# Seven block products in place of eight for the second layer of the last 32 steps instead of the last 24

## The reference

```
xW = einsum('ntd,dg->ntg', x, Wx) + b                 # 256 -> 1024
a = xw_t + prev_h @ Wh                                # per step, 256 -> 1024
next_c = sigmoid(f) * prev_c + sigmoid(i) * tanh(g)
next_h = sigmoid(o) * tanh(next_c)

h = concatenate([h, -h], axis=-1)
h = s0 * (h @ sign(k0)); h = relu(h) * 2              # 512 -> 1024
h = s1 * (h @ sign(k1)); h = relu(h) * 2              # 1024 -> 1024
h = s2 * (h @ sign(k2))                               # 1024 -> 256
y = x + h
```

## Time and profile before

| | |
|---|---|
| median of 3 runs | 272.96 us (272.89 to 273.32) |
| the profiled execution | 273.06 us, of it 271.2 us from the first to the last instruction |
| TensorE busy | 267.2 us of the 271.2 (99%), 3568 matmuls |
| VectorE, ScalarE, GpSimd busy | 215.4 us, 174.6 us, 48.1 us |
| the first step of the recurrence begins | 19.09 us |
| the last piece of fill ends, the part behind the loop begins | 223.02 us |
| granted TensorE clock | 1.00 |

### The profile page before, as it was taken

How to read it: one execution, slowest core, us unless ns; L and a number is a source line. 1 busy time by engine, 2 the same in 40 slices (tenths; PEclk the granted TensorE clock), 3 DMA queues, 4 the chain that set the end, 5 groups by cost and what they waited for, 6 DMA issues and landing times.

```text
span 271.2 us, 8903 instructions
## 1 busy us (share of the span) xinstructions
PE 267.2 (99%) x3568; PEld 219.9 (81%) x3568; DVE 215.4 (79%) x769; ACT 174.6 (64%) x522; POOL 48.1 (18%) x70
## 2 busy tenths in 40 slices
PE   8999999999999999999999999999999999999995
PEld 6888888878999999999998899998887676666563
DVE  3878888888888888888888888887777777997355
ACT  4789786878566667655765576556777867733320
POOL 0010000012211112331222102000222225603030
PEclk9999999999999999999999999999999999999999
DMA  7980000000000000000010001000000010100003
GB/s 210 346 342 1 4 2 0 2 4 2 2 0 4 4 2 22 22 2 5 2 42 0 2 4 41 2 2 4 4 0 2 2 42 0 41 0 0 2 0 116
DMA packets 5432, 8.72 MB, mean 32 GB/s; under 512 B 656, under 2 KB 3472, under 8 KB 5264
## 3 DMA queue, kind: packets, MB, share of 16 engines
q1 hardware_dynamic: 5104, 7.64, 8.1%
q10 hardware_dynamic: 288, 0.52, 0.5%
HBM read 6.07 MB, written 2.10 MB: 30 GB/s over the span
## 4 chain that ended last, share of the span: by engine, by line
PE 98%; DVE 1%; POOL 0%; issue 0%; POOLq 0%
PE WK L555 36%; PE WK L538 14%; PE G L517 11%; PE WK L573 10%; PE G L508 10%; PE ACC L587 6%; PE G L573 4%; PE WK L604 2%; PE ACC L604 1%; PE G L649 1%; PE G L538 1%; PE ACC L538 1%; DVE x L886 1%; PE G L555 0%; POOL zero L1094 0%
## 5 line engine op out<-in xcount | busy, mean ns | idle before, releaser
L555 PE MATMUL WK<-h,k 128*128 128x256 f16 (+1 forms) x856 | 107.7, 276 | 0.0
L555 PEld LDWEIGHTS WK<-h,k 128*128 128x128 fp8e5 x856 | 80.8, 98 | 11.3 <-issue 0.2
L814 ACT ACTIVATE tT<-aT 128x128 f32<-128x128 f32 x126 | 39.0, 310 | 44.6 <-DVE aT L1033 43.4
L1033 DVE TENSOR_REDUCE aT<-G 128x128 f32<-128x256 f32 x128 | 48.2, 418 | 7.7 <-PE G L517 6.3
L701 ACT ACTIVATE G<-xw 128x256 f32<-128x256 f32 x126 | 46.6, 370 | 0.0
L538 PE MATMUL WK<-xs,wxs 128*128 128x512 f32 x168 | 42.5, 400 | 0.0
L517 PE MATMUL G<-h,w 128*128 128x64 f16 x1008 | 39.5, 192 | 0.0
L508 PEld LDWEIGHTS G<-h,w 128*128 128x128 f16 x1008 | 32.9, 96 | 6.7 <-DVE h L1050 5.1
L538 PEld LDWEIGHTS WK<-xs,wxs 128*128 128x128 f32 x168 | 30.4, 188 | 5.9
L508 PE MATMUL G<-h,w 128*128 128x32 f16 x1008 | 35.2, 177 | 0.0
L517 PEld LDWEIGHTS G<-h,w 128*128 128x128 f16 x1008 | 33.2, 97 | 0.0
(11 more groups left out here) (116 smaller groups left out, 283.9 us busy)
## 6 DMA issues: line engine op xcount, KB each, us to landing
x<-in_x SPq DMA_DIRECT2D x3, 512.0 KB, 8.4
out_y<-x SPq DMA_DIRECT2D x10, 128.0 KB, 1.8
xw<-in_wh SPq DMA_DIRECT2D x4, 256.0 KB, 5.0
k<-in_k SPq DMA_DIRECT2D x1, 1024.0 KB, 10.2
out_y<-x SPq DMA_DIRECT2D x4, 192.0 KB, 1.9
x<-in_x ACTq DMA_DIRECT2D x2, 256.0 KB, 3.6
xw<-in_wx SPq DMA_DIRECT2D x4, 128.0 KB, 4.0
xw<-in_wx SPq DMA_DIRECT2D x2, 256.0 KB, 5.2
```

Of the source, the lines that this page charges most:

```text
L555: ins = eng.matmul(layer_src(tile), w, rhs, start=a == 0, stop=last)
L814: eng.activation(tT[:, B * j0:B * j1], aT[:, j0:j1].rearrange("p j b -> p (j b)"), ACT.Tanh, scale=half_gain0 if t == 0 else half_gain).th ...
L1033: eng.tensor_reduce(aT[:, j0:j1], G[g][:, 0:256].rearrange("p (j h b) -> p j b h", h=2, b=B), op=ALU.add, axis=AX.X).then_inc(added[g])
```

## The change

The portions become four of 8 steps and two of 16 steps, so that the seven products cover the last 32 steps. A wide portion has 512 columns, a whole PSUM bank. With this:

- `N1`, `N2` are 4 and 5, `NW` is 512; the second layer of steps 32 to 39, which was a portion of its own with 128 matmuls of 256 columns, is now part of the seven products;
- `fill(t)` is 2.03 for every step from 1 on, where it was 2.2 to 2.3;
- the first layer of portion `N1` is spread over other steps, and p1 and p2 change places with its last tiles; one matmul of p2 moves behind the loop;
- the terms tq of products 5 and 6, and t23, move from xw and h1 to memory that xs and wxs leave free, and those of product 4 into b1; ScalarE waits for the last x product or for p2 before it writes them;
- h1 keeps a size of its own, and the copies of p1 wait for the seed of step 39 instead of step 31.

```
-CHUNKS = ((0, 8), (8, 8), (16, 8), (24, 8), (32, 8), (40, 12), (52, 12))
-N1, N2 = 5, 6
+CHUNKS = ((0, 8), (8, 8), (16, 8), (24, 8), (32, 16), (48, 16))
+N1, N2 = 4, 5
...
 def fill(t):
-    return 3.4 if t < 0 else 1.8 if t < 1 else 2.3 if t < 9 else 2.2 if t < 16 else 2.3
+    return 3.4 if t < 0 else 1.8 if t < 1 else 2.03
...
 def act_cost(tile):
-    return 0.48 if tile[0] == "y" else 0.67 if tile[0] == "x" else 0.95 if tile[:2] == (0, N1) else 0.38
+    return 0.48 if tile[0] == "y" else 0.67 if tile[0] == "x" else 1.3 if tile[:2] == (0, N1) else 0.38 if tile[0] in (0, 1) else 0.67
...
-    return {"mix": 0.65, "y": 0.74, 0: 0.93}[chore[0]]
+    return {"mix": 0.65, "y": 0.74, 0: 1.25}[chore[0]]
...
-        at = (2, 2, 3, 4, 5, 6, 6, 7) if c == 0 else (0, 1, 2, 3, 4, 5, 6, 6) if c < N1 - 1 else (1, 2, 3, 4, 5, 6, 6, 7)
+        at = (2, 2, 3, 4, 5, 6, 6, 7) if c == 0 else (0, 1, 2, 3, 4, 5, 6, 6) if c < N1 - 1 else (3, 4, 5, 6, 7, 7)
...
-    return order + [((f"p{q}", m), 8) for q, m in ((1, 0), (1, 1), (1, 2), (2, 0), (1, 3), (2, 1), (2, 2), (2, 3))]
+    for tile in (("p1", 0), (0, N1, 6), ("p1", 1), (0, N1, 7), ("p1", 2), ("p2", 0), ("p1", 3), ("p2", 1), ("p2", 2), ("p2", 3)):
+        order.append((tile, matmuls(tile)))
+    return order
...
-                empty_at[tile] = 1.6 + 2.2 * (tile[2] % 4) + (1.7 if tile[2] < 4 else 3.4)
+                empty_at[tile] = 1.6 + 2.8 * (tile[2] % 4) + (2.1 if tile[2] < 4 else 4.2)
...
-        xs = sb("xs", [P, 2, 2, 2, 512], F32R)
-        wxs = sb("wxs", [P, 2, 2, NJ, 128], F32R)
+        with nc.sbuf_tensor("xs", [P, 2, 2, 2, 512], F32R) as xs, nc.sbuf_tensor("wxs", [P, 2, 2, NJ, 128], F32R) as wxs:
+            pass
+        t23 = sb("t23", [P, 2, 4, NW], F32)
+        tq01 = sb("tq01", [P, 2, 4, 2, NW], F16)
...
-        tq = cut(xflat[:, 22 * NW:38 * NW].bitcast(F16), 0, 4, 4, 2, NW)
-        b22 = cut(xflat[:, 38 * NW:42 * NW].bitcast(F16), 0, 4, 2, NW)
+        b22 = cut(xflat[:, 22 * NW:26 * NW].bitcast(F16), 0, 4, 2, NW)
+        tq = [tq01[:, 0], tq01[:, 1], cut(xflat[:, 26 * NW:30 * NW].bitcast(F16), 0, 4, 2, NW), b1[:, 0:4]]
...
             def term_hi(i, k):
                 e.wait_ge(t_made[i], k + 1)
-                eng.activation(tq[:, i, k, 0], term(i, k), ACT.Copy).then_inc(t_hi[i])
+                if i < 2:
+                    e.wait_ge(x_mm, 4 * NJ)
+                elif i == 3:
+                    e.wait_ge(prod_mm[2], 4)
+                eng.activation(tq[i][:, k, 0], term(i, k), ACT.Copy).then_inc(t_hi[i])
```

## The result

| | before | after |
|---|---|---|
| median of the runs compared | 273.14 us (272.89 to 273.93) | 282.14 us (281.79 to 282.31) |
| span of the profiled execution | 271.2 us | 280.2 us |
| first step begins | 19.09 us | 19.43 us |
| part behind the loop begins | 223.02 us | 218.14 us |
| TensorE busy | 267.2 us, 3568 matmuls | 273.5 us, 3376 matmuls |

The ratio of after to before is 1.0323, with an interval of 1.0298 to 1.0347: 3.2% slower, with 192 matmuls fewer. The forecast was 281.3 us.

The account below looks back on a forecast made before the run. The recurrence's 3.06 us a step was to bound the loop after the change: -2.2 (matmuls) + 7.9 (floor) + 2.7 (VectorE), less 0.2 of small waits, + 0.2 (end) = +8.4 on 272.96, 281.3 us; range 279.0 to 284.0.

Parts of the forecast that it names:

- main step: In the loop: a recurrence step takes at least 3.06 us whatever its fill, while TensorE's work is 2.93 us a step.
- Matmuls: TensorE's work by count: 16.1 us less in the loop, 13.9 more behind it, together 2.2 us less.
- Waiting in the loop: TensorE waiting for h in nearly every step: 7.9 us from the floor and 2.7 from VectorE.
- VectorE's pairs: Between h and the reduce: two tiles add 0.08 us a step with one older, 0.12 with both fresh.
- p2 tile of step 61: In step 61, emptying a 512-column p2 tile puts the reduce about 1.2 us behind L1050, costing 0.3 us.
- The end: From the last matmul, 3.1 us: grows 0.1 us for the wider y_add and 0.1 for the 256 KB output.
- "some 10 us" of waits: Sign in the profile after: TensorE's weight loads released by VectorE's h in nearly all steps, some 10 us in total.
- Wide tiles late: Rival: wide 512-column tiles cost 0.2 us in each of eight steps and 0.7 behind the loop; 283.6 us, 8%.
- Faster than before: Rival: the recurrence gives way, less loaded steps run in 2.94 us or less, TensorE stays the bound; 271.0 us, 4%.
- The clock: Rival: TensorE's pauses lower its clock, 2.8 us more for each such step; four give 292.5 us, 3%.
- the pauses of its stretch: From 51.2 to 60.7 us: TensorE waited 0.27 and 0.39 us for h, among 256-column matmuls, with the clock at 1.00.

Follow-up runs that it names:

- the pair of runs with the shorter chain: Both kernels with the new cell in one VectorE instruction instead of two, an equal one issued behind h's low part: after 272.33 us, before 272.84 us.
- The run with short low parts: Kernel after with the low part of VectorE's layer tiles cut from 256 to 64 columns, matmuls reading high parts instead: 280.11 us.
- the first run of 28 steps: Kernel after with portions 8, 8, 8, 8, 4, 14, 14 and fill 2.28, 2.26, 2.21 us: 279.98 us, ratio 1.0238 to the kernel before.
- one with a fill of 2.3: Kernel after, 32 steps, with a fill of 2.3 us a step instead of 2.03: 298.12 us, ratio 1.0903.
- 28 steps, second run: Kernel after with portions 8, 8, 8, 8, 4, 14, 14, p1 and p2 later, fill 2.11, 2.23, 2.29, 2.21, 2.11 us: 277.16 us, ratio 1.0132.
- 32 steps, tuned: Kernel after with fill 2.11, 2.10, 2.07, 2.09, 2.06 us and the first layer's wide tiles at other places: 281.71 us, ratio 1.0305.
- 26 steps, first plan: Kernel after with portions 8, 8, 8, 8, 6, 13, 13 and fill 2.33, 2.22, 2.25, 2.31, 2.24 us: 277.63 us, ratio 1.0146.

## Why the prediction was right

Its main step was that a step of the recurrence cannot be shorter than 3.06 us, whatever the fill, and that 187.5 us of loop work over 64 steps lies below that. The steps after are 3.06 to 3.07 us apart without a pair, h releases TensorE in 63 of 63, and the pair of runs with the shorter chain shows that it is this chain that held them.

Term by term:

- Matmuls: -2.2 us expected. Behind the loop 58.76 us were measured (218.14 to 276.90), with 288 matmuls; the 58.95 of the prediction are for 289, of which one ran before 218.14. A matmul of 512 columns takes 3.45 / 16 = 0.2156 us, where 0.2158 was worked out from two other widths:

```profile
250.99 3.45 PE G L576 x16
```

- Waiting in the loop: 10.6 expected (7.9 for the floor, 2.7 for VectorE), 11.0 measured. VectorE's pairs were sized right for each step: 3.13 us, 0.07 more than 3.06, with one older tile, 3.17 to 3.18 with two fresh ones, and 3.46 with the two tiles and w2_make behind h of step 15. The run with short low parts puts the tiles at 2.0, and the two steps with w1_make (3.19 each) add 0.25. The floor itself is 3.066 rather than 3.06 us (37 steps of that run take 113.5 us), which is 0.4 us over 62 steps. One step (187.22 to 190.42) took 3.20 us, because VectorE's f32 copy of h began 0.27 us behind h instead of 0.14; the run with short low parts has the same step, and its cause stays open.
- One part of it was wrong in kind. The p2 tile of step 61 was to make the reduce 0.3 late. ScalarE had its high part ready early, and the reduce came 0.92 behind h, hardly later than the 0.90 of the floor (211.81 to 212.73). It was 1.18 only behind step 62 (214.88 to 216.06), where TensorE no longer waits:

```profile
212.13 0.68 DVE L884 SCALAR_TENSOR_TENSOR h<-WK,h 128x512 f16<-128x512 f32 x1
...
212.73 0.75 DVE L1040 TENSOR_REDUCE aT<-G 128x128 f32<-128x256 f32 x2
...
215.45 0.69 DVE L884 SCALAR_TENSOR_TENSOR h<-WK,h 128x512 f16<-128x512 f32 x1 [0.17 <-ACT h L731]
...
216.06 0.74 DVE L1040 TENSOR_REDUCE aT<-G 128x128 f32<-128x256 f32 x2
```

- Missing in the sum: ScalarE in the first steps. In step 4 it had a part of x and two input tiles to empty, and the next tanh had to wait for it:

```profile
31.66 0.63 ACT L687 ACTIVATE xs<-x 128x512 fp32r<-128x512 f32 x1
...
32.20 1.25 ACT L696 ACTIVATE xw<-WK,biasS 128x512 f32<-128x512 f32 x2
33.34 0.51 ACT L821 ACTIVATE tT<-aT 128x128 f32<-128x128 f32 x2
```

The step took 3.30 us (31.66 to 34.96). With step 2 (3.18) that is 0.3 us, the same kind of loss as VectorE's: TensorE's longer fill took 3.27 us in these steps before, and covered it.

- The end: 0.2 us expected; from the last matmul to the end 3.3 us were measured, against 3.1 in the prediction's reading and 3.0 in the trace before, with 2.1 us for an output of 256 KB.
- The rest of the difference, 0.3 us, is the first step, which began at 19.43 us. It lay between 19.10 and 20.03 us in the other traces, whose kernels load the same inputs, and the latest was a variant of the kernel before. So nothing shows that it belongs to the change.
- The sign of "some 10 us" of waits was right for the loop, 11.0 us by its balance, and not for the weight loads that it named: they stood idle for 22.1 us, in part while matmuls were still running.

Of the rivals, none came about. Wide tiles late: steps 57 to 60 are 3.06 to 3.07 us each. Faster than before would have needed the chain to give way, and it is made of latencies that didn't.

The clock stayed at 1.00 with waits in all 63 steps. The Trainium skill ("TensorE: Matmul & The Clock Gate", section "A second HAM failure mode: psum-queue depth-cycling") tells of a clock that swings where the engine pauses briefly and often between groups of matmuls. With pauses as short as these the trace does not agree. The pauses of 0.5 to 1.1 us in the first run of 28 steps are nearer to it: the clock fell there. The prediction's remark that the pauses of its stretch were of 256-column matmuls is not quite right, since 7 of the 11 fill matmuls of step 11 were f32 ones with 512 columns; but f16 matmuls of 512 columns stand in the kernel after only from step 50 on. So the price of a fallen clock was near: plans not far from this one paid 1.7 us for it, and one with a fill of 2.3 paid 13.9.

## What to carry to other kernels

Where one engine makes up 98% of the chain and a recurrence runs beside it, look for a step in which that engine waited, and read the recurrence's own period there; the distance to it is all that taking away work can gain. Work that moves from beside the recurrence to behind it is paid in full once the loop is at that floor: here 15.9 us left the loop, which became 5.2 us shorter, and 13.6 us came back behind it. In a plan made by hand, the sum of steps has to hold four things besides the steps: the operands that another engine makes for the fill, the last step's own latency, the surcharges that a longer fill hid, and the clock, which fell in three of the plans that left TensorE without work.

## What the runs showed of the hardware

In the kernel after, TensorE's granted clock stayed at 1.00 although its weight loads stood idle for h before every one of 63 steps, 0.35 us on average and 0.7 at most. It also stayed at 1.00 through a single gap between matmuls of 1.7 us (28 steps, second run) and through gaps of 0.9 and 1.4 us in two steps that follow each other (32 steps, tuned). It fell to 0.60 and 0.79 in the 5.7 us behind a single gap of 2.1 us (26 steps, first plan). And it fell to 0.58 and 0.85 in 213 to 219 us of the first run of 28 steps, behind gaps of 1.08, 0.47 and 1.00 us, none of them as long as the 1.4 and 1.7 us that left it alone. So the longest gap does not tell whether the clock falls; what does is not shown here. Each of these two falls cost 1.7 us of matmul time by estimate. With a fill of 2.3, where gaps of up to 2.1 us came again and again, it cost 13.9 us.
